# Pairs of maxima placed by slot width, four of them moved to the experts, first half's projection and routing later

## What is computed

```python
h = layernorm(x) * (1 + ca) + sa
x = x + ga * attention(h)          # 16 heads, q and k of 16 content + 32 RoPE values,
                                   # keys and values from a latent of rank 64 (RMS normed),
                                   # queries from one of rank 128, causal softmax over 1024 tokens
h = layernorm(x) * (1 + cb) + sb
x = x + gb * experts(h)
# experts: h = h @ Wm + bm, cut into 8 parts of 32 values; each part has its own routing:
# logits = t @ emb (16 experts), softmax, the two best; gelu(t @ W1[e] + b1) @ W2[e] + b2
# weighted by them; the parts joined again, @ Wo + bo
```

## Time and profile before

| | us |
|---|---|
| median of 3 runs | 3072.03 (3066.36 to 3072.98) |
| the profiled execution | 3070.06 |
| its span, first to last instruction | 3068.3 |
| busy in the span: PE / DVE / ACT / POOL | 2880.1 / 1908.1 / 1804.0 / 1320.1 |
| mean granted clock of TensorE | 0.97 |

### The profile page before, as it was taken

The page is one execution under the profiler, slowest core; times in us unless marked ns, Lnnn a source line. Parts: engine busy times, 40 slices in busy tenths (PEclk is TensorE's granted clock), DMA queues, the critical chain, the costliest instruction groups (busy, mean ns, idle before and its releaser), DMA issues.

```text
span 3068.3 us, 51536 instructions
## 1 busy us (share of the span) xinstructions
PE 2880.1 (94%) x16460; PEld 1276.4 (42%) x16460; DVE 1908.1 (62%) x4637; ACT 1804.0 (59%) x2146; POOL 1320.1 (43%) x1355
## 2 busy tenths in 40 slices
PE   5689999999998999999999999999999999998999
PEld 2243444444444444444444444444444444444433
DVE  5465766757657566665666656665656747657453
ACT  1145665556754667546674466654766556754686
POOL 3312465225552364514644246532465225552254
PEclk8699999999999999999999999999999999999999
DMA  5201453024530344204442054310453123530242
GB/s 137 43 25 32 120 137 87 26 59 114 135 91 1 94 110 128 67 1 108 118 109 65 7 128 122 102 41 25 124 135 87 29 57 103 138 87 16 67 127 90
DMA packets 176245, 252.54 MB, mean 82 GB/s; under 512 B 50797, under 2 KB 82557, under 8 KB 175885
## 3 DMA queue, kind: packets, MB, share of 16 engines
q1 hardware_dynamic: 168988, 247.26, 31.2%
q10 hardware_dynamic: 6996, 1.99, 0.3%
HBM read 159.13 MB, written 12.63 MB: 56 GB/s over the span
## 4 chain that ended last, share of the span: by engine, by line
PE 85%; DVE 6%; issue 3%; ACT 1%; POOL 0%; SPq 0%; DMA 0%; POOLq 0%; ACTq 0%; DVEq 0%
PE ps L1248 18%; PE ps L1211 17%; PE ps L1266 16%; PE ps L1232 9%; PE ps L412 8%; PE ps L458 4%; PE ps L510 2%; PE ps L529 2%; PE ps L499 2%; PE ps L460 2%; DVE front L555 2%; PE ps L486 1%; PE ps L517 1%; PE ps L444 1%; PE ps L468 1%
## 5 line engine op out<-in xcount | busy, mean ns | idle before, releaser
L1332 ACT ACTIVATE rest<-ps 128x1024 f32<-128x1024 f32 x1024 | 992.8, 1022 | 370.5 <-PE ps L1248 368.7
L1314 ACT ACTIVATE rest<-ps 128x1024 f32<-128x1024 f32 (+3 forms) x768 | 608.3, 810 | 649.9 <-PE ps L1211 638.5
L1419 POOL TENSOR_TENSOR rest<-rest 128x512 f32<-128x512 f32 x480 | 630.0, 1313 | 650.5 <-DVE rest L1368 644.0
L1248 PE MATMUL ps<-wide,w1s 98*128 98x512 f32 x2048 | 623.8, 425 | 11.3 <-ACT rest L1332 8.5
L552 DVE CUSTOM_DVE_ANT_0 rest<-ps,maskd 128x128 f32<-128x128 f32 (+3 forms) x1024 | 460.7, 488 | 223.4 <-PE ps L412 215.4
L1409 POOL TENSOR_SCALAR_AFFINE_SELECT rest<-rest 128x256 f32<-128x256 f32 x512 | 211.0, 420 | 888.3 <-ACT rest L1314 885.2
L1266 PE MATMUL ps<-rest,w2s 128*32 128x512 f32 x4096 | 547.1, 606 | 0.6 <-ACT rest L1332 0.6
L1248 PEld LDWEIGHTS ps<-wide,w1s 98*128 98x128 f32 x2048 | 339.7, 188 | 492.6 <-ACT rest L1332 354.9
L1368 DVE SCALAR_TENSOR_TENSOR rest<-ps,b2c,wide 128x512 f32<-128x512 f32 x512 | 382.5, 747 | 260.1 <-PE ps L1266 233.6
L1211 PE MATMUL ps<-wide 49*128 49x512 f32 (+3 forms) x2304 | 500.7, 523 | 5.4 <-ACT rest L1314 4.9
L555 DVE TENSOR_REDUCE front<-ps 128x1 f32<-128x512 f32 x512 | 329.6, 685 | 211.7 <-PE ps L412 207.2
(11 more groups left out here) (136 smaller groups left out, 2292.0 us busy)
## 6 DMA issues: line engine op xcount, KB each, us to landing
wide<-gate_rows SPq DMA_DIRECT2D x1024, 128.0 KB, 2.8
wide<-front SPq DMA_DIRECT2D x480, 64.0 KB, 2.0
wide<-front SPq DMA_DIRECT2D x192, 128.0 KB, 2.3
ao<-in_x SPq DMA_DIRECT2D x16, 512.0 KB, 5.1
heads<-front SPq DMA_DIRECT2D x64, 128.0 KB, 2.4
xs<-in_x SPq DMA_DIRECT2D x16, 512.0 KB, 4.9
out<-xs SPq DMA_DIRECT2D x16, 512.0 KB, 3.4
wide<-ao SPq DMA_DIRECT2D x96, 64.0 KB, 2.3
```

The lines of the kernel that those rows point to most:

```text
L1248: mm = pe.matmul(bank(2 * (u % 2) + k), L.w1s[:, e, :], L.x2[:, c, 4 * j + 2 * p + k, :], start=True, stop=True)
L1314: nc.scalar.activation(L.pt[:, u % PTS, :, f:HALF], L.ps[:, 2 * (u % 2):2 * (u % 2) + 2, 0:HALF - f], ACT.Exp, scale=SCALE).then_inc(S["c_ ...
L1332: nc.scalar.activation(L.hm[:, u % HM, :], bank(2 * (u % 2), 2), ACT.Gelu).then_inc(S["e_gelu"], 1)
L1419: g.tensor_tensor(dst, dst, L.gy[:, k % GY, :], ALU.add).then_inc(S["e_add"], 1)
```

## The change

`attend_slots` gets a table `PLACES` for the images from 1 on: for each pair a slot and whether it stands between the score phases (0) or behind them (1). Slots of 384 to 512 mostly keep two pairs, those of 256 and 128 have mostly one. The first four pairs of group 1's second half (`AHEAD`) are no longer in attention but in the last four steps of the experts before; to make room the pairs of groups 0 and 1 in the experts begin two and three steps earlier, in steps 36 and 52. Where a slot has a RoPE item and a pair behind, the RoPE item comes first. In all images the first half's `tr`, `o`, `stats`, `xn`, `tr2`, `tm`, `tlo`, `lg` and `chain` move to later slots.

```diff
--- before.py
+++ after.py
@@ -1048,30 +1048,43 @@
 NQ = NU // 2
 
 
+AHEAD = 4
+PLACES = [(0, 1), (1, 0), (2, 0), (3, 0), (4, 0), (4, 1), (5, 0), (7, 0), (8, 0), (8, 1)]
+PLACES += [(s, part) for s in range(9, 15) for part in range(2)] + [(15, 0), (15, 1)]
+PLACES += [(16, 0), (16, 1), (17, 0), (17, 1), (18, 0), (19, 0), (20, 0), (20, 1), (21, 0), (21, 1), (22, 0), (23, 0)]
+PLACES += [(s, part) for s in range(24, 30) for part in range(2)] + [(30, 0), (31, 0)]
+PLACES += [(s, part) for s in range(32, 37) for part in range(2)]
+
+
 def attend_slots(img):
 
 
     slots = [([], [], []) for _ in range(NM)]
     if img:
         slots[1][1].extend([("out", 2), ("out", 3)])
-    if img:
-        pairs = [(s, ("pair", 1, *p)) for s, p in zip((0, 2, 3, 4, 5, 6, 7, 8), PAIRS[1])]
-        pairs += [(9 + k // 2, ("pair", 2, *p)) for k, p in enumerate(PAIRS[0])]
-        pairs += [(13 + k // 2, ("pair", 3, *p)) for k, p in enumerate(PAIRS[0])]
-        pairs += [(17 + k // 2, ("pair", 1, *p)) for k, p in enumerate(PAIRS[1][8:])]
+        places = PLACES
+        pairs = [("pair", 1, *p) for p in PAIRS[1][AHEAD:AHEAD + 10]]
+        pairs += [("pair", g, *p) for g in (2, 3) for p in PAIRS[0]]
+        pairs += [("pair", 1, *p) for p in PAIRS[1][AHEAD + 10:]]
+        pairs += [("pair", g, *p) for g in (2, 3) for p in PAIRS[1]]
     else:
-        pairs = [(k * 7 // 16, ("pair", 0, *p)) for k, p in enumerate(PAIRS[1])]
-        pairs += [(9 + k // 3, ("pair", 2, *p)) for k, p in enumerate(PAIRS[0])]
-        pairs += [(12 + k // 3, ("pair", 3, *p)) for k, p in enumerate(PAIRS[0])]
-        pairs += [(15 + k * 6 // 16, ("pair", 1, *p)) for k, p in enumerate(PAIRS[1])]
+        places = [(k * 7 // 16, 0) for k in range(16)] + [(9 + k // 3, 0) for k in range(8)]
+        places += [(12 + k // 3, 0) for k in range(8)] + [(15 + k * 6 // 16, 0) for k in range(16)]
+        places += [(21 + k // 2, 0) for k in range(32)]
+        pairs = [("pair", 0, *p) for p in PAIRS[1]] + [("pair", g, *p) for g in (2, 3) for p in PAIRS[0]]
+        pairs += [("pair", g, *p) for g in (1, 2, 3) for p in PAIRS[1]]
         slots[7][0].append(("rmax", 0))
         slots[7][1].append(("row", 0, 1))
-    pairs += [(21 + k // 2, ("pair", 2, *p)) for k, p in enumerate(PAIRS[1])]
-    pairs += [(29 + k // 2, ("pair", 3, *p)) for k, p in enumerate(PAIRS[1])]
-    for s, pair in pairs:
-        slots[s][1 if s == 0 or slots[s][0] else 0].append(pair)
-    for k, s in enumerate((0, 2, 3, 4, 5, 6, 7, 8)):
-        slots[s][1].append(("rope", 8 + k))
+    assert len(places) == len(pairs)
+    ropes = {s: ("rope", 8 + k) for k, s in enumerate((0, 2, 3, 4, 5, 6, 7, 8))}
+    for (s, part), pair in zip(places, pairs):
+        if img == 0 and slots[s][0]:
+            part = 1
+        if part and img and s and s in ropes:
+            slots[s][1].append(ropes.pop(s))
+        slots[s][part].append(pair)
+    for s, rope in ropes.items():
+        slots[s][1].append(rope)
     for s, g in ((21, 1), (29, 2), (37, 3)):
         slots[s][0].insert(0, ("rmax", g))
     for s, row in ((13, (2, 0)), (17, (3, 0)), (21, (1, 1)), (29, (2, 1)), (37, (3, 1))):
@@ -1079,18 +1092,18 @@
     for m, gc in enumerate(SEQ[:-1]):
         last = max(s for s, step in enumerate(MAIN) if step[:2] == gc)
         slots[last + 2][2].append(("sums", m))
-    slots[26][1].append(("tr", 0, 0))
-    slots[27][1].append(("tr", 0, 1))
-    slots[28][1].append(("o", 0, 0))
-    slots[29][1].extend([("o", 0, 1), ("stats", 0)])
-    slots[31][1].append(("xn", 0))
-    slots[33][1].extend([("tr2", 0, 0), ("tr2", 0, 1)])
-    slots[34][1].append(("tm", 0, 0))
-    slots[35][1].extend([("tm", 0, 1), ("tlo", 0, 0)])
-    slots[36][1].extend([("tlo", 0, 1), ("lg", 0), ("chain", 0, 1), ("chain", 0, 2)])
-    slots[38][1].append(("exp", 0))
+    slots[27][1].append(("tr", 0, 0))
+    slots[28][1].append(("tr", 0, 1))
+    slots[32][1].append(("o", 0, 0))
+    slots[33][1].extend([("o", 0, 1), ("stats", 0)])
+    slots[34][1].append(("xn", 0))
+    slots[35][1].extend([("tr2", 0, 0), ("tr2", 0, 1)])
+    slots[36][1].append(("tm", 0, 0))
+    slots[37][1].extend([("tm", 0, 1), ("tlo", 0, 0)])
+    slots[38][1].extend([("tlo", 0, 1), ("lg", 0), ("chain", 0, 1), ("chain", 0, 2)])
+    slots[39][1].append(("exp", 0))
     for k in range(3, 18):
-        slots[37 + (k - 3) // 2][1].append(("chain", 0, k))
+        slots[40 + (k - 3) // 3][1].append(("chain", 0, k))
     slots[45][2].append(("gt", 0))
     return slots
 
@@ -1141,12 +1154,14 @@
     at(37, ("kc", 1))
     for k, p in enumerate(PAIRS[0]):
         at(28 + k, ("pair", 0, *p))
-        at(55 + k, ("pair", 1, *p))
+        at(52 + k, ("pair", 1, *p))
     for k, p in enumerate(PAIRS[1]):
-        at(38 + k, ("pair", 0, *p))
+        at(36 + k, ("pair", 0, *p))
+    for k, p in enumerate(PAIRS[1][:AHEAD]):
+        at(60 + k, ("pair", 1, *p))
     at(36, ("row", 0, 0))
     at(54, ("row", 0, 1))
-    at(63, ("row", 1, 0))
+    at(62, ("row", 1, 0))
     return slots
 
 
```

## The result

The change makes the kernel faster: the median of five runs is 3042.05 us (3033.82 to 3046.17), against 3067.67 us (3064.24 to 3072.98) for the kernel before on the same chip. The ratio is 0.9909, 95% interval 0.9891 to 0.9927.

A forecast was written before the change was run, and what follows sets the result against it. TensorE, busy 94% of the span, was taken to bound the kernel. Attention waits and pairs -43, attention clock -20, experts' banks +50, experts' clock +12 made -1 us on 3070.06; forecast 3071 us, range 3044 to 3096.

The forecast's parts named there:

- Attention: clock: All eight attentions: TensorE's half clock goes, half of its loss counted; 20 us less, ends 0 and 22.
- Attention waits: Attention of images 1 to 7, per image: 6.8 us of waits go, 1.6 come, 0.8 is not gained.
- the moved matmuls: Four pairs of score products leave each attention of images 1 to 7 for the experts before: 1.4 us an image.
- The waits named: TensorE's waits for maxima in attention, in slots such as 19 (0.65 us), 30 (0.98) and 32 (2.92), taken as gone.
- The floor: Attention slots 19, 23 and 31 shrink only to 1.06 us, as scores wait for ScalarE; 0.8 us an image not gained.
- Attention: waits that come: Fill and normalisation meet in slot 34; new waits in slots 34 and 35, 1.6 us an image, ends 0.3 and 4.
- Experts: the ring of two banks: Experts' steps 36, 37, 54, 62, 63: items wait for banks 6 and 7; 50 us more, ends 10 and 55.
- Experts: clock: Experts: the new waits bring one fall to half clock per image, 12 us more, ends 0 and 35.
- The routing later: First half's routing and expert-input DMAs run later in attention, still ahead of the experts: no cost.
- the clock stays up: Rival: no clock falls in the experts, all 22 us back in attention; -15 us, 3057 us; chance 0.25.
- The profile after: Expected profile: attention of images 1 to 7 near 165 us, 4 to 5 idle; experts of images 0 to 6 203 to 205.

The follow-up runs named there:

- Experiment 2: The kernel before with only the first half's projection, normalisation and routing in later slots, all pairs as before: 3022.03 us, ratio 0.9843.
- experiment 3: The changed kernel with the first half's projection, normalisation and routing back in their old slots, pairs as changed: 3080.89 us, ratio 1.0047.
- experiment 4: Two edits of the changed kernel: GpSimd's fill later in its program, which moved nothing, 3035.14 us; the fill waiting for the four normalisations, 3029.08 us.
- Experiments 1 and 5: 1: the changed kernel without the four moved pairs, their maxima not computed, 2981.83 us; 5: the changed kernel with the pair first in steps 36 and 54, 3028.76 us.

## Why the prediction was wrong

The forecast was no change, a sum of -1 us; the two profiled executions differ by -28.0.

- **"Attention: clock" is the step that failed.** It said "20 us less", from the clock column's 0.98 of 172.6 us, "part of that fell on idle time, so I count half". Nearly all of the half clock fell on busy time: 61.3 of 64.9 us in images 1 to 7, since it begins behind a wait or near its end. It gave back 30.7 us there and 3.0 in image 0, so 34 instead of 20, which is above the term's upper end of 22. That is half of what the forecast missed. Experiment 2 shows that the shift of the projection did this, experiment 3 that the pairs did not. The stage's mean was good enough: 8 x 3.5 + 8.6 = 36.6 us. The halving took 14 off, and reading when the clock fell (1350.0, 1360.2) and which matmuls took double time would have shown that there was nothing to halve.
- **Attention waits.** "6.8 - 1.6 - 0.8" an image, so 4.4 less idle: measured 32.8 / 7 = 4.7. With the moved matmuls and image 0's 2.1 us of idle that makes 45 us against the forecast's 43. The waits named did go: slot 19's, slot 30's and slot 32's. The floor is there too: slots 19, 23 and 31 last 1.07 us, forecast 1.06. The 6 us that no row holds come on top.
- **"Attention: waits that come": right in mechanism and size.** The fill and the normalisation met in slot 34 (L626 from 1356.01, the fill's end 1354.57 + 3.51 = 1358.08), and slot 35's pair waited 0.88, forecast 0.7; experiment 4 removed it by parting the two. The 0.65 forecast for slot 34 was 0.84; the 0.25 for slot 35's transposes does not show. In all 1.7 us against 1.6.
- **"Experts: the ring of two banks": right.** "50 us more" against 33.6 + 9.8 + 4 = 47. Step 36 was forecast 2.4 us longer and is 2.3, step 37 2.05 and 2.07, step 54 2.1 and 1.93, steps 62 and 63 0.65 and 0.63 (at full clock). Experiments 1 and 5 show the cause. There are two waits for L654, as forecast, and one for L685, of 1.25 us in image 3 behind half clock and 1.56 in image 0 at full clock, where 1.6 was forecast.
- **"Experts: clock": right in size.** "12 us more" against 9.6: the time at half clock rose from 13.7 to 34.1 us in seven stages, 3.4 to 10.2 us in each. One fall an image was charged; at steps 36 and 37 it came in five of seven. The section of the Trainium skill that the forecast cites (TensorE: Matmul & The Clock Gate, "Why this matters for your kernels") would have had none, as none of these waits is longer than 1.6 us; the trace does not agree, with 23.9 us at half clock behind them.
- **The routing later** cost nothing, as forecast: experiment 2 moves it and its experts last what they did.
- **The forecast's signs** were right for each of its terms, and no miss hid another: the clock of attention was short by 14 us, its waits and matmuls by 8 (the 6 without a row among them), the experts too dear by 3 and their clock by 2. The rival nearest to the result, "the clock stays up" (3057), took the whole clock term of attention, 22 us, where 34 came, and the experts' clock term as 0; the experts' falls came, and the attention was underestimated still.
- **The profile after:** attention "near 165" is 162.5, since the clock had cost more; idle "4 to 5" is 5.9 (the forecast's own terms give 10.6 - 4.4 = 6.2), "no wait over 1 us" holds, the experts at 203 to 205.7 are as said.

What stays open: 6 us in attention and 4 in the experts that neither idle time, matmuls nor clock account for; matmul ends are modelled in the trace. Experiment 2 has only 0.6 of the 6, so they come with the spread of the pairs. Every fall in the attentions before stands in a wait or within 0.9 us behind it, but no run changes one wait and nothing else and gains or loses a fall by it, so what decides whether one follows is open. Why the falls of the clock differ between executions of one kernel is not settled either.

## What to carry to other kernels

A wait costs more than its length when half clock follows it (before the change 30.7 us in seven attentions): take the time at which the clock fell, look at which wait stands just ahead, and charge the busy time behind it, not a share of the stage's mean. Work that shares a ring of banks should be weighed by who empties the bank it needs, not by how long its matmuls take: four pairs with 1.4 us of matmuls cost 8 us a stage in the experts (57 / 7), where their banks were still being read, and 2.1 in attention, where they stood in slots with room. An order of instructions that moves an item past nothing that waits moves nothing in time: the trace, not the diff, says whether an experiment was made.

## What was not expected of the hardware

GpSimd's fill of 3.51 us, which writes SBUF, held back VectorE's normalisation (L626, SBUF in and out): in all eight images of the changed kernel the first of the four took 2.22 us and ended 0.15 us after the fill, and 0.4 us in the kernel of experiment 4 that parts them. VectorE's masked maxima, which read PSUM and the mask in SBUF, were not slowed: L552 of 384 columns took 0.55 or 0.56 us under the fill and without it. The Trainium skill (SBUF — State Buffer, "Who interferes with whom") calls the port pair that GpSimd shares with VectorE an exclusive lock for some of VectorE's instructions: whoever comes second waits until the other's instruction ends. The trace agrees, with the 0.15 us above.

The clock falls at different places from run to run of the same kernel. The kernel with the ineffective edit of experiment 4 had a profiled execution of 3057.47 us and a median of 3035.14; these are two expert stages of that execution, images 3 and 4:

```profile
1408.22:1613.42 205.20, 196.10 (x1043) 86.60 (x1043) 130.82 (x289) 139.76 (x158) 108.10 (x83) 0.98 0.45 115
1775.92:1983.10 207.18, 198.41 (x1043) 87.81 (x1043) 130.74 (x289) 139.89 (x158) 108.14 (x83) 0.97 0.44 114
```

Idle time in its seven expert stages is 62.7 us as in the changed kernel, the time at half clock 61.4 instead of 34.1. And waits of one length are not alike. In the experts half clock followed waits of 0.88 and 0.76 in step 36 of images 1, 2 and 3, and the same waits in images 4 and 6 had none behind them. In experiment 2 it followed a wait of 0.53 in slot 30 in one attention of seven; in no attention of images 1 to 7 after the change did it follow the 0.84 and 0.88 of slots 34 and 35, which stand 5 us apart.
